# Turning the softmax probabilities on the DMA crossbar instead of on TensorE, in a three-layer graph attention kernel

## The reference

```
h = relu(layernorm0(x))                        # without scale and shift
for l in 0, 1, 2:
    si, sj  = h @ attn_w[l, :256], h @ attn_w[l, 256:]
    scores  = leaky_relu(si[:, :, None] + sj[:, None, :] + attn_b[l], 0.2)
    attn    = softmax(where(adj + eye > 0, scores, -inf))
    g       = layernorm(h + attn @ h) * g1[l] + beta1[l]
    ff      = gelu(g @ W1[l] + b1[l]) @ W2[l] + b2[l]
    h       = layernorm(g + ff) * g2[l] + beta2[l]
out = x + h
```

## Time and profile before

| | us |
|---|---|
| median of 3 runs (lowest, highest) | 2337.41 (2336.14, 2338.91) |
| the profiled execution | 2337.64 |
| its span, first to last instruction | 2335.8 |
| PE busy (share) | 2243.3 (96%) |
| ACT busy | 1899.7 (81%) |
| POOL busy | 1863.4 (80%) |
| DVE busy | 1791.5 (77%) |
| ScalarE's L507, first and last of 96 | 38.66, 2242.07 |
| mean granted TensorE clock | 0.993 of full speed |

### The profile page before, as it was taken

One profiled execution on the slowest core, in us unless ns is written; L12 is line 12 of the kernel. 1 busy time (PEld: TensorE's weight loads), 2 busy tenths in 40 slices (PEclk: granted clock), 3 DMA queues, 4 the chain that ended last, 5 costly groups with the idle time before them and its releaser, 6 DMA issues.

```text
span 2335.8 us, 46423 instructions
## 1 busy us (share of the span) xinstructions
PE 2243.3 (96%) x15840; PEld 1570.0 (67%) x15840; DVE 1791.5 (77%) x5889; ACT 1899.7 (81%) x3496; POOL 1863.4 (80%) x1640
## 2 busy tenths in 40 slices
PE   2799999999999999999999999999999999999996
PEld 2466776776666776767666767677666677767764
DVE  5777777778887777778888777777888777777763
ACT  3788888888888888888888888888888888888873
POOL 1468778788998787878898878787989887877886
PEclk9999999999999999999999999999999999999998
DMA  5331111114342110112443101011344110111233
GB/s 156 104 69 28 24 24 24 24 26 97 87 101 59 24 28 19 28 19 55 100 93 93 33 19 28 20 28 21 80 105 100 33 28 19 28 24 24 42 77 82
DMA packets 280169, 121.11 MB, mean 52 GB/s; under 512 B 209792, under 2 KB 278400, under 8 KB 279936
## 3 DMA queue, kind: packets, MB, share of 16 engines
q1 hardware_dynamic: 263040, 101.37, 18.6%
q0 software_dynamic: 16896, 16.78, 4.7%
HBM read 51.01 MB, written 16.78 MB: 29 GB/s over the span
## 4 chain that ended last, share of the span: by engine, by line
PE 79%; DVE 10%; ACT 6%; issue 3%; DMA 1%; SPq 0%; POOL 0%; POOLq 0%; ACTq 0%
PE p_hid L377 35%; PE p_pair L391 35%; PE p_pair L437 4%; PE p_pair L415 2%; DVE g_lo L571 2%; DVE bn L578 2%; PE p_pair L423 1%; DVE res L652 1%; ACT probs L513 1%; ACT p_hid L478 1%; DMA x_in<-in_x 1%; DVE res L673 1%; ACT L478 1%; ACT L513 1%; DVE adj_in L599 1%
## 5 line engine op out<-in xcount | busy, mean ns | idle before, releaser
L571 DVE TENSOR_TENSOR g_lo<-p_hid,g_hi 128x512 f16<-128x512 f32 x768 | 528.9, 689 | 478.5 <-ACT g_hi L483 471.8
L391 PE MATMUL p_pair<-w_hi,g_hi 128*128 128x256 f16 x3072 | 837.9, 273 | 0.0
L391 PE MATMUL p_pair<-w_lo,g_hi 128*128 128x256 f16 x3072 | 837.8, 273 | 0.0
L391 PE MATMUL p_pair<-w_hi,g_lo 128*128 128x256 f16 x3072 | 837.8, 273 | 0.0
L478 ACT ACTIVATE p_hid<-p_hid,b_eff 128x512 f32<-128x512 f32 x768 | 504.4, 657 | 296.8 <-PE p_hid L377 295.4
L777 POOL TENSOR_TENSOR rstd<-var_eps,minus_half 128x4 f32<-128x4 f32 x224 | 236.5, 1056 | 397.9 <-DVE minus_mean L586 387.0
L483 ACT ACTIVATE g_hi<-p_hid 128x512 f16<-128x512 f32 x768 | 458.5, 597 | 24.3
L377 PE MATMUL p_hid<-hT_hi,w_hi 128*128 128x512 f16 x1536 | 458.8, 380 | 3.9 <-DVE g_lo L571 2.0
L377 PE MATMUL p_hid<-hT_lo,w_hi 128*128 128x512 f16 x1536 | 458.4, 380 | 0.5 <-DMA hT_lo<-h_lo 0.3
L377 PE MATMUL p_hid<-hT_hi,w_lo 128*128 128x512 f16 x1536 | 458.6, 380 | 0.0
L391 PEld LDWEIGHTS p_pair<-w_lo,g_hi 128*128 128x128 f16 x3072 | 300.6, 98 | 106.8
(11 more groups left out here) (66 smaller groups left out, 3492.6 us busy)
## 6 DMA issues: line engine op xcount, KB each, us to landing
x_in<-in_x SPq DMA_DIRECT2D x32, 512.0 KB, 3.7
w_f<-in_x POOLq DMA_DIRECT2D x32, 512.0 KB, 5.8
out<-w_f SPq DMA_DIRECT2D x32, 512.0 KB, 4.9
adj_in<-in_adj SPq DMA_DIRECT2D x32, 256.0 KB, 4.2
w_f<-in_L_gnn_W SPq DMA_DIRECT2D x6, 1024.0 KB, 6.8
hT_hi<-h_hi SPq DMA_TRANSPOSE x96, 3.1
hT_lo<-h_lo SPq DMA_TRANSPOSE x96, 3.1
attn_rows<-in_L_gnn_attn_w SPq DMA_DIRECT2D x1, 768.0 KB, 6.0
```

The lines of the kernel that those rows point to most:

```text
L391: mm = pe.matmul(ff_banks(s)[:, t, :], g[i][:, nodes], w[l][:, c, :], start=(c == 0 and t % 2 == 0 and n == 0), stop=(c == C - 1 and n == ...
L571: dve.tensor_tensor(g_lo[i][:], p_hid[k][:], g_hi[i][:], ALU.subtract).then_inc(g_lo_ready, 1)
```

## The change

The probabilities are split before they are turned. ScalarE makes p_hi from `probs` right behind the exponentials, in chunk 5 of the slot of item s + 3; DVE makes p_lo in chunk 0 of the next slot, behind that chunk's g_lo and ahead of `aggregates`, and the reciprocal of the sums goes there with it. SyncE turns both by DMA transpose into pT_hi and pT_lo, the low half ahead of `turn_h` and the high half of the item after it behind `turn_h`. TensorE's transposes, ScalarE's copy and DVE's subtraction from PSUM in chunk 4 are gone. `aggregate` waits for the two transfers.

```diff
-        pT_hi, pT_lo = sb("pT_hi", [P, TN], F16), sb("pT_lo", [P, TN], F16)
+        p_hi, p_lo = sb("p_hi", [P, T, N], F16), sb("p_lo", [P, T, N], F16)
+        pT_hi, pT_lo = sb("pT_hi", [P, T, N], F16), sb("pT_lo", [P, T, N], F16)
...
+            def turn_probs_lo(r, s):
+                sp.wait_ge(p_lo_ready, total(r, s, 1, 1))
+                if later(r, s):
+                    sp.wait_ge(agg_ready, total(r, s - 1, 1, 1))
+                sp.dma_start_transpose(pT_lo[:], p_lo[:].rearrange("p t n -> p (t n)")).then_inc(pT_lo_ready, 16)
+
+            def turn_probs_hi(r, s):
+                sp.wait_ge(p_hi_ready, total(r, s, 1, 1))
+                if later(r, s):
+                    sp.wait_ge(agg_ready, total(r, s - 1, 1, 1))
+                sp.dma_start_transpose(pT_hi[:], p_hi[:].rearrange("p t n -> p (t n)")).then_inc(pT_hi_ready, 16)
...
+                if is_item(r, s + 2):
+                    turn_probs_lo(r, s + 2)
                 if is_item(r, s + 1):
                     turn_h(r, s + 1)
+                if is_item(r, s + 3):
+                    turn_probs_hi(r, s + 3)
...
-            def transpose_probs(r, s):
-                pe.wait_ge(probs_ready, total(r, s, 4, 4))
-                if later(r, s, 3):
-                    pe.wait_ge(res2_ready, total(r, s - 3, 2, 2))
-                for t in range(T):
-                    mm = pe.transpose(pT_bank(s)[:, t, :], probs[:, t, :], ident[:])
-                mm.then_inc(pT_psum, 1)
...
-                pe.wait_ge(pT_lo_ready, total(r, s, 1, 1))
+                pe.wait_ge(pT_hi_ready, total(r, s, 16, 16))
+                pe.wait_ge(pT_lo_ready, total(r, s, 16, 16))
...
-                    if c == 4 and is_item(r, s + 2):
-                        transpose_probs(r, s + 2)
...
+                    act.wait_ge(p_lo_ready, total(r, s - 1, 1, 1))
                 for t in range(T):
                     act.activation(probs[:, t, :], leaky[:, t, :], ACT.Exp, bias=minus_max[:, t:t + 1],
                                    accum_out=row_sum[:, t:t + 1]).then_inc(probs_ready, 1)
 
-            def copy_probs(r, s):
-                act.wait_ge(pT_psum, total(r, s, 1, 1))
-                act.activation(pT_hi[:].rearrange("p (t n) -> p t n", n=N), pT_bank(s), ACT.Copy).then_inc(pT_hi_ready, 1)
+            def high_probs(r, s):
+                act.wait_ge(probs_ready, total(r, s, 4, 4))
+                if later(r, s):
+                    act.wait_ge(pT_hi_ready, total(r, s - 1, 16, 16))
+                act.activation(p_hi[:], probs[:], ACT.Copy).then_inc(p_hi_ready, 1)
...
-                    if c == 4 and is_item(r, s + 2):
-                        copy_probs(r, s + 2)
                     if c == 5 and is_item(r, s + 3):
                         exponentials(r, s + 3)
+                        high_probs(r, s + 3)
...
             def low_probs(r, s):
-                dve.wait_ge(pT_hi_ready, total(r, s, 1, 1))
-                dve.tensor_tensor(pT_lo[:].rearrange("p (t n) -> p t n", n=N), pT_bank(s),
-                                  pT_hi[:].rearrange("p (t n) -> p t n", n=N), ALU.subtract).then_inc(pT_lo_ready, 1)
+                dve.wait_ge(p_hi_ready, total(r, s, 1, 1))
+                if later(r, s):
+                    dve.wait_ge(pT_lo_ready, total(r, s - 1, 16, 16))
+                dve.tensor_tensor(p_lo[:], probs[:], p_hi[:], ALU.subtract).then_inc(p_lo_ready, 1)
...
+                    if c == 0 and is_item(r, s + 2):
+
+                        low_probs(r, s + 2)
+                        row_sums(r, s + 2)
                     if c == 0 and is_item(r, s + 1):
                         aggregates(1, total(r, s + 1, 10, 8))
...
-                    if c == 4 and is_item(r, s + 2):
-                        low_probs(r, s + 2)
-                        row_sums(r, s + 2)
```

More of the change, by code:

```diff
@@ L227, in sj_bank @@
             return p_pair[s % 2][:, 0:2, :].rearrange("p a (u n) -> p (a u) n", n=N)
-        def pT_bank(s):
-            return agg_banks(s)[:, 2:4, :].rearrange("p a (u n) -> p (a u) n", n=N)
         attn_dma, rows_dma, cols_dma = sem("attn_dma"), sem("rows_dma"), sem("cols_dma")
@@ L251, in gnn_kernel @@
         sum_steps = sem("sum_steps")
-        pT_psum = sem("pT_psum")
+        p_hi_ready = sem("p_hi_ready")
+        p_lo_ready = sem("p_lo_ready")
         pT_hi_ready = sem("pT_hi_ready")
@@ L434, in aggregate @@
                 for t in range(T):
-                    nodes = slice(t * N, (t + 1) * N)
                     for n, (p, v) in enumerate(((pT_hi, X_hi), (pT_hi, X_lo), (pT_lo, X_hi))):
-                        mm = pe.matmul(agg_banks(s)[:, t, :], p[:, nodes], v[:, t, :],
+                        mm = pe.matmul(agg_banks(s)[:, t, :], p[:, t, :], v[:, t, :],
                                        start=(n == 0), stop=(n == 2))
```

## The result

The changed kernel takes 2372.44 us (median of 4 runs, 2371.39 to 2373.64), the kernel before 2337.33 in the same comparison: ratio 1.015, 95% interval 1.0132 to 1.0168. It is 1.5% slower, clear of the noise. The forecast was 2367, its range 2350 to 2396.

What follows compares the result with a forecast made beforehand. A hidden loop through ScalarE, VectorE and GpSimd, not PE, was to become the bound: 88 intervals +26.3 us, start +4, end -1, span 2335.8 + 29.3 = 2365.1, so 2367 us, 1.3% slower; range 2350 to 2396.

Steps and rivals of the forecast that it cites:

- the hidden loop: Plain slots: a loop through ScalarE, DVE and GpSimd, 22.42 us, only 0.6 us shorter than the slot.
- ScalarE, the copy: Between exponentials and table load: the new copy adds 0.63 us to the loop, bounds 0.48 to 0.96.
- VectorE, -0.68 and +0.68: Subtraction and reciprocal leave chunk 4 (-0.68 us) and return in chunk 0 (+0.68 us), both on the loop.
- the fourth rival: The port: low_probs always waits for a GpSimd instruction, 0.7 us in each of 95 slots, 2433 us; 7%.
- Plain slot: Layers 1 and 2: the loop becomes the bound, 23.05 us against 23.02; PE's 0.44 us turns into idle time.
- Full slot: Layer 0 with mask, statistics and normalised input: loop through ScalarE and VectorE, 24.02 + 0.76 = 24.78 us.
- Statistics alone: Full slot without the mask: loop of 22.86 us, hidden behind PE's 23.02, becomes 23.62.
- between: Three intervals between the kinds of slot: from about 23.6 us to 24.20.
- Transfers: Two more DMA transposes per slot: both have over 7 us; hT_lo lands later but fits with 0.8 to spare.
- (1): Whole kernel: PE, 96% busy, bounds it, so its 0.44 us per slot is gained, 2295 us; 5%.
- (2): Before the table load: copy falls into a drain paid anyway, cost 0, 2320 us; 5%, plus 4% for a mixture.
- (3): Crossbar late: two more turns push hT_lo 1 us past its need, every plain slot grows, 2422 us; 6%.

Runs made afterwards that it cites:

- e2_high_c7: Changed kernel with ScalarE's copy making p_hi moved from behind the exponentials to behind chunk 7's g_hi: 2325.79 us, 0.9956 of the kernel before.
- e6_copy_twice: Changed kernel with a second ScalarE copy of the probabilities, into an unused buffer, ahead of the first: 2421.36 us (two runs), 1.0364 of the kernel before.
- e1_low_c5: Changed kernel with DVE's low half made in chunk 5 behind the dot products, its turn behind the high one: 2319.91 us, 0.993 of the kernel before.
- e4_spare_turns: Changed kernel with four unused transposes of the identity put back on PE in chunk 4: 2377.28 us, 1.0178 of the kernel before.
- e5_off_spare: e3_both_off with four unused transposes put back on PE in chunk 4: 2347.94 us, 1.005 of the kernel before.
- e3_both_off: Changed kernel with the copy behind chunk 7's g_hi, low half and reciprocal behind chunk 2's residual: 2318.01 us, 0.9923 of the kernel before.
- e7_turn_twice: Changed kernel with the high half turned twice by DMA, once into an unused buffer: 2371.78 us, 1.0149 of the kernel before.

## Why the prediction was right, and where it was not

**What bounds the kernel, and the hidden loop: right.** The loop of 22.42 us, taken from a catch-up interval, is confirmed: with its two additions off it, plain slots fall to PE's 22.59 (forecast for PE alone 22.58), and to 22.43 in the first slots of `e2_high_c7`, where that loop is seen again at its old length. Added up from 22.42 with the terms as measured (copy +0.65, chunk 4 -0.68, low half +0.60, reciprocal +0.09), the loop's length comes out in four kernels: 23.08 in after (measured 23.09), 22.43 without the copy (22.43), 22.48 without the low half (22.49), 21.74 without all three (21.76).

**ScalarE, the copy: right, 0.65 for 0.63.** `e2_high_c7` removes it alone: plain slots 23.09 to 22.43, while PE's floor is at 22.59 once it has no reserve left. `e6_copy_twice` adds one: +0.53, since only the last copy before the table load pays its full length.

**VectorE, -0.68 and +0.68: right in plain slots.** L670 takes 0.68 and 0.60 from start to start, the reciprocal 0.09. `e1_low_c5` takes it out of chunk 0 and the plain slot falls to 22.49, as 23.09 - 0.60 says. It did not meet GpSimd there, so the fourth rival falls where the change put it; in `e1_low_c5` it does and lasts 2.17 in full slots.

**Plain slot: right.** 23.09 against 23.05. PE's 0.44 us became waiting; `e4_spare_turns` puts them back at no cost (0.01), `e5_off_spare` shows that where PE bounds they cost 0.43.

**Full slot: the number nearly right (24.69 for 24.78), the mechanism wrong.** The step that failed is "Its loop runs through mask, L578 of the input, L673, L415, chunk 4's hidden matmuls and L633", and so the sum + 0.63 + 0.68 - 0.55. The 24.02 from which the sum starts already held a wait: the mask lasted 1.37 in place of its 0.68, because it ended only when h_res had ended. That makes a second loop, mask, minus_mean, GpSimd's series, h_res, mask, and it is this one that sets the full slot, before and after. In that loop the copy has no part (`e2_high_c7`, `e6_copy_twice`: 24.69 in both), nothing comes back at chunk 4, and the low half with the reciprocal is all: + 0.67. Of the three terms, +0.68 is right and the other two do not belong there; that +0.63 and -0.55 nearly cancel, so that the sum was 0.76, is luck. For the expectations of `e2_high_c7` and `e3_both_off`, which built on the same loop, the error was open: 0.65 and 1.0 us per full slot.

**Statistics alone 23.53 to 23.55 (forecast 23.62), between 24.24 to 24.48 (24.20), mask alone 23.67 to 23.72 (23.68): right** within 0.1 for most. The third slot with statistics alone of each round, which stands before the full ones, took 23.76 to 23.95, one of the "between" 24.48. Slots with statistics alone do follow the loop that was drawn for the full ones (`e4_spare_turns`).

**Transfers: right in plain slots, wrong in others and at the end.** Both new turns have time to spare (`e7_turn_twice`). The turn of h_lo takes 3.1 us to land as before, but it is issued later. In the 55 plain slots PE waits for it once, in the last but one (0.87 at 2235.78), and that slot is no longer than the others; "0.8 to spare" held. In slots of layer 0 and next to them PE waits for hT_lo 17 times, 0.28 to 1.00 us, where before it waited once (0.30). In the full slots, where the other loop bounds, this does not show in the time; for the slots next to them no run tells. In the last slots there is nothing to spare either. Timeline of PE in after, two slots:

```profile
2281.63 0.60 PE L391 MATMUL p_hid<-hT_lo,w_hi 128*128 128x512 f16 x2 [0.50 <-DMA hT_lo<-h_lo]
...
2304.57 0.60 PE L391 MATMUL p_hid<-hT_lo,w_hi 128*128 128x512 f16 x2 [0.62 <-DMA hT_lo<-h_lo]
```

So the end, forecast at -1, was +1.3: PE arrives earlier at a transfer that comes later. The two waits are 1.1 us; where the rest of the 2.3 came from is not shown.

**Total.** Forecast minus measured: 88 intervals 2066.7 against 2067.24, start +4 against +5.7, end -1 against +1.3. Of the 5.4 us by which the median is above the forecast, 0.5 are the loop, 1.7 the start, 2.3 the end; the rest is the distance of the profiled execution's span and the median (2369.6 and 2372.44, 2.8 against the 1.8 that I used). The start and the end are from one execution each, and the mark at the start moved by 1.3 and 1.5 us in two kernels whose edits were not meant for the start (208.67 in `e7_turn_twice`, 208.87 in `e4_spare_turns`), so these terms are good to about that. The range was added up wrongly at its top: 2396 is for the costliest copy alone, and with a start of 10 it would be 2402.

**The rivals.** PE's time is not gained (1). The copy does not fall into a drain (2): load 0.65 after the copy's start. The crossbar is not late (3) in the plain slots that were to show it; PE's waits for it stand in slots of layer 0, at the start and at the end. The port (4) did not meet L670 but had bounded the full slots before the change, by the mask.

## What to carry to other kernels

An engine that is 96% busy is the bound only by the slack of the next loop: measure that slack (here 0.6 us of 23) by a marker that occurs once per period, and by a stretch in which the kernel catches up, before taking work off the busy engine. What a moved instruction costs is decided by its place: the same copy and subtraction gave 2372 us between the exponentials and the table load and ahead of the statistics, and 2318 where their engines mostly waited anyway. Ask of each instruction that is moved what waits behind it, and of each instruction whose length varies from slot to slot for whom it is waiting.

## What the runs showed of the hardware

A DVE instruction with two inputs in SBUF that met one of GpSimd's long tensor-tensor instructions (h_res, X_lo, L829, L831) stretched until 0.53 to 0.58 us after that instruction's end: the mask beside h_res 17 times before, 19 in after and 19 in `e2_high_c7`, the subtraction 87 times in `e1_low_c5`. Alone both take 0.68; stretched, the mask took 0.82, 1.36, 1.90 and 2.04 in the kernels shown, the subtraction 0.97, 1.43 and 2.17. GpSimd's next instruction, into which they ran, was longer as well: rstd 1.49 for 1.01 behind the mask, h_res 2.69 for 2.35 and L831 1.60 for 1.27 behind the subtraction. Beside GpSimd's last normalisation, in mask-only slots of before, the mask kept its 0.68, and GpSimd's four instructions took 2.87 in place of 2.17. I had expected a cost of fractions of a microsecond; what I had not expected is that such a wait can close a loop between two engines that pass each other no data at that place, and that it absorbs what a third engine gains: full slots of 24.69 us with the copy once, twice, or out of the way.

A DMA transpose of a 128 x 512 float16 tile landed 2.4 us after its issue, beside 1.19 us for the issue itself; a third one of the probabilities per slot changed neither its neighbours by more than 0.1 us nor the time of the kernel (2371.78 against 2372.44).
